# Two attentions: row maxima two groups ahead, and the first mask moved from TensorE to VectorE

## The chip, the cores and the metric

The program runs on one core of one Trainium2 chip. The metric is the device time of one launch in microseconds (us), and lower is better.

## The reference

Four blocks follow each other on x of shape (8, 256, 256), each added to x: an attention over a context with a causal mask, a mixture of 16 experts with the two best per token, a second attention over the same context without a mask, and a mixture of 7 experts with a capacity and a shared expert. What matters here are the two attentions, each with 16 heads of 16 channels and 256 queries and 256 keys per batch element:

```python
scores = jnp.einsum('bhqd,bhkd->bhqk', q, k) / jnp.sqrt(jnp.float32(dk))
causal = jnp.triu(jnp.ones((q_len, k_len), dtype=bool), k=1)
scores = jnp.where(causal, NEG_INF, scores)          # first attention only
scores = jnp.where(attention_mask[:, None, :, :], NEG_INF, scores)
attn = jax.nn.softmax(scores, axis=-1)
out = jnp.einsum('bhqk,bhkd->bhqd', attn, v)
```

## The kernel before

`attend_block` builds one attention. It runs over 8 batch elements, called batches here, and in a batch over 4 groups (`NG`) of 4 heads (`G`), so 32 groups per attention. The five engines are programmed apart and meet at semaphores; the order of the work is written out by hand in one function `batch` for each engine. All engines execute their instructions in order.

Queries and keys are split in three bf16 parts each (`split`, on VectorE for the first ones, on GpSimd after that), stored to DRAM (`store_parts`) and loaded back as stacks of 96 rows (`load_stack`, 12 transfers of 128 KB per batch: 6 of `ks<-parts` and 6 of `qs<-parts`). There are two stacks, used in turn: the loads for batch f go into the stack that batch f-2 used, so SyncE waits for the last transposed scores of batch f-2 (semaphore `scoredT`) and for the stores of the parts before it issues them. In the middle of batch n TensorE also makes the keys, queries and values of batch n+2 and the output of batch n-1, spread over the 16 heads ("slots") by `feed`. The queries of batch n+2 are made in slots 7 and 8, taken by ScalarE in slot 9 and then split by GpSimd.

Each group goes through these steps.

- `score` (TensorE, L984 and L986): scores with queries on the partitions, from the 96 rows. It writes one unit at a time into two PSUM banks used in turn; a unit is four heads by 128 keys or two heads by 256 keys, 3 units per group in the first attention and 4 in the second. In the first attention each product is followed by a second matmul that adds the mask `shut` through an identity.
- `reduce` (VectorE, L639): one `tensor_reduce` per unit takes the row maxima into PSUM. A unit may be scored when the reduce of the unit two before it is done (`reduced`).
- `tops` (VectorE, L647 and L649): splits the maxima in two bf16 parts.
- `turn_tops` (TensorE, L997): transposes them into a PSUM bank that the transposed scores use too.
- ScalarE copies them as rows 96 to 104 of the stack of queries (L882).
- `scoreT` (TensorE, L1016 and L1018): per head the scores with keys on the partitions, from 104 rows, so that the row maximum is subtracted by the matmul; in the first attention the mask is added by a second matmul. Two banks in turn.
- ScalarE takes the exponential (L892), `value` (TensorE, L1032) multiplies by the values, ScalarE copies out (L855, `take`), `turn_o` (TensorE) transposes, `normalize` (VectorE, L658 to L664) divides by the sum.

Before the change these run one group apart: in group g, TensorE scores the units of group g+1 and turns the maxima of group g. Its order within a group is the one of the lines below; `more` is false in the last group alone.

```python
score_next(0)
turn_tops(at)
if started:
    value(prior(at))
score_next(1)
scoreT(at, 0)
...
scoreT(at, 3)
```

Since `score_next` in group 3 belongs to the next batch, the stack of that batch is waited for there (`stacks_loaded`). In the first batch of the first attention VectorE also takes the moments (`moments`, L627) of the tiles to come, and their averages close its group 1; GpSimd waits for them (`root`), and the split of the queries of batch 2 stands behind that.

## Time and profile before

| | us |
|---|---|
| runs of the kernel, median (lowest, highest) | 1265.51 (1264.04, 1271.85) |
| profiled execution, span from first to last instruction | 1262.1 |
| first attention, about | 0 to 220 |
| second attention, about | 500 to 693 |

| engine | busy us | share of the span |
|---|---|---|
| TensorE, matmul | 1123.7 | 89% |
| TensorE, weight load | 974.6 | 77% |
| VectorE | 690.8 | 55% |
| ScalarE | 595.9 | 47% |
| GpSimd | 360.7 | 29% |

The span comes from one execution taken with the profiler, and it has no other time of its own; what lies around the instructions is taken as the difference to the median, 3.4 us. Busy times of matmuls overlap each other, so a high share does not say how much a matmul costs; the distance between two starts does.

### The profile page before, as it was taken

What the parts mean: (1) busy time and instruction counts of PE and PEld (TensorE: products, weight loads), DVE (VectorE), ACT (ScalarE), POOL (GpSimd) and SP (SyncE); (2) the same over time, 40 slices, a digit from 0 to 9 for tenths busy, and PEclk for the clock granted to TensorE, in tenths of its full rate; (3) what the DMA queues carried; (4) which work ended last, traced back from release to release, by engine and by line L of the source; (5) the groups of instructions that cost most, each with busy time, mean ns of one, the idle gap of its engine ahead of it and who ended that gap; (6) DMA issues with size and microseconds to landing.
All of it is one profiled execution on the core that took longest, in us unless ns stands there. A gap on an engine that the chain in (4) does not pass through costs nothing. (4 is left out here: it accounts for less than half of the span.)

```text
span 1262.1 us, 25941 instructions
## 1 busy us (share of the span) xinstructions
PE 1123.7 (89%) x8539; PEld 974.6 (77%) x8539; DVE 690.8 (55%) x1558; ACT 595.9 (47%) x1211; POOL 360.7 (29%) x502
## 2 busy tenths in 40 slices
PE   5999998739999984888998679999999999999997
PEld 4788786329888873555665379999999999999996
DVE  4755666652222226676767655555556555555556
ACT  3566666313222222776787334444445444444432
POOL 6566650112222205776630145000000000000261
PEclk8899999859999996999999879999999999999999
DMA  7774461548999957568471221223232232232132
GB/s 182 175 180 120 129 179 37 193 159 292 332 330 325 314 207 163 111 136 146 89 125 24 100 89 59 79 63 112 72 103 76 87 109 87 86 100 73 50 97 80
DMA packets 88137, 172.56 MB, mean 137 GB/s; under 512 B 11251, under 2 KB 59949, under 8 KB 81792
## 3 DMA queue, kind: packets, MB, share of 16 engines
q1 hardware_dynamic: 71712, 136.15, 39.0%
q0 software_dynamic: 9584, 29.32, 7.9%
q10 hardware_dynamic: 6768, 6.16, 1.4%
q8 instruction: 40, 0.66, 0.2%
q14 instruction: 33, 0.27, 0.1%
HBM read 133.11 MB, written 39.20 MB: 137 GB/s over the span
## 5 line engine op out<-in xcount | busy, mean ns | idle before, releaser
L2136 PE MATMUL e_ps<-xT_e,wp_e 128*128 128x384 f32 (+1 forms) x1344 | 245.2, 331 | 4.0 <-DVE wp_e L2010 4.0
L2136 PEld LDWEIGHTS e_ps<-xT_e,wp_e 128*128 128x128 f32 x1344 | 221.7, 188 | 5.4 <-issue 4.1
L639 DVE TENSOR_REDUCE att_ps<-att_ps 128x2 f32<-128x512 f32 (+1 forms) x224 | 155.3, 697 | 103.5 <-PE att_ps L986 63.2
L1968 ACT ACTIVATE act_a_e<-e_ps 128x256 f32<-128x256 f32 (+2 forms) x176 | 77.8, 442 | 159.9 <-PE e_ps L2136 150.9
L2066 DVE TENSOR_TENSOR hid_e<-act_a_e,e_ps 128x256 f32<-128x256 f32 (+2 forms) x176 | 87.0, 494 | 116.6 <-ACT act_a_e L1968 102.4
L892 ACT ACTIVATE probs<-att_ps 128x384 f32<-128x384 f32 (+1 forms) x256 | 130.4, 546 | 41.4 <-PE att_ps L1018 29.0
L1972 ACT ACTIVATE hidp_e<-hid_e 128x256 fp32r<-128x256 f32 (+2 forms) x176 | 83.8, 476 | 127.3 <-DVE hid_e L2066 121.5
L2153 PE MATMUL e_ps<-wp_e,hidp_e 128*128 128x256 f32 (+1 forms) x1008 | 138.4, 282 | 2.9 <-DVE xres L2026 1.2
L2068 DVE TENSOR_TENSOR hidp_e<-hid_e,hidp_e 128x256 fp32r<-128x256 f32 (+2 forms) x176 | 87.8, 499 | 95.5 <-ACT hidp_e L1972 90.1
L2153 PEld LDWEIGHTS e_ps<-wp_e,hidp_e 128*128 128x128 f32 (+1 forms) x1008 | 130.7, 183 | 4.9 <-issue 4.1
L1608 ACT ACTIVATE hid_e<-e_ps,b_ahead 128x128 f32<-128x128 f32 x188 | 53.7, 368 | 139.9 <-PE e_ps L1713 129.2
L1919 POOL DMA_DIRECT2D done<-y_e x7 | 6.2, 893 | 384.3 <-DVE y_e L2050 384.3
L984 PE MATMUL att_ps<-ks,qs 96*128 96x256 bf16 (+1 forms) x512 | 102.4, 267 | 11.4 <-DMA qs<-parts 9.5
L2136 PE MATMUL e_ps<-xT_e,swp_e 128*128 128x256 f32 x768 | 106.0, 289 | 1.5 <-issue 0.8
L1016 PE MATMUL att_ps<-qs,ks 104*128 104x256 bf16 (+1 forms) x512 | 99.7, 262 | 3.4 <-ACT qs L882 1.5
L1713 PEld LDWEIGHTS e_ps<-xT_e,w_e 128*128 128x128 f32 x752 | 89.9, 194 | 16.5 <-issue 15.3
L2136 PEld LDWEIGHTS e_ps<-xT_e,swp_e 128*128 128x128 f32 x768 | 98.5, 195 | 2.8 <-DVE swp_e L2005 2.3
L1713 PE MATMUL e_ps<-xT_e,w_e 128*128 128x128 f32 x752 | 94.4, 279 | 6.4 <-DMA w_e<-in_W 5.8
L1589 POOL DMA_INDIRECT x_e<-rows,owner_e x47 | 44.7, 952 | 168.7 <-PE e_ps L1703 125.1
L882 ACT ACTIVATE qs<-att_ps 8x1024 bf16<-8x1024 f32 x64 | 65.1, 1017 | 52.9 <-PE att_ps L997 52.0
L1722 PE MATMUL e_ps<-w_e,hid_e 128*128 128x256 f32 x376 | 88.9, 380 | 0.0
L984 PEld LDWEIGHTS att_ps<-ks,qs 96*128 96x128 bf16 x512 | 48.0, 100 | 39.7 <-issue 20.7
(235 smaller groups left out, 1850.0 us busy)
## 6 DMA issues: line engine op xcount, KB each, us to landing
w_e<-in_W SPq DMA_DIRECT2D x47, 1024.0 KB
w_e<-in_W SPq DMA_DIRECT2D x57, 384.0 KB, 3.1
ks<-parts SPq DMA_DIRECT2D x96, 128.0 KB, 4.7
qs<-parts SPq DMA_DIRECT2D x96, 128.0 KB, 5.2
parts<-cut SPq DMA_DIRECT2D x30, 384.0 KB, 3.2
x_e<-rows SPq DMA_DIRECT2D x8, 768.0 KB, 5.6
done<-y_e ACTq DMA_DIRECT2D x47, 128.0 KB
rows<-zeros POOLq DMA_DIRECT2D x8, 736.5 KB, 6.6
```

The source lines that it names most:

```text
L639: dve.tensor_reduce(tops_at(at[3])[:, qt, x0:x0 + heads], src, AX.X, ALU.max).then_inc(reduced, 1)
L892: act.activation(probs[:, g % 2, x0, 0:WIDE], ps[:, TB + x0 % RING, 0:WIDE], ACT.Exp, scale=DK ** -0.5).then_inc(exped, 1)
L984: last = pe.matmul(out, qs[0:KS, j, hd, qt * P:(qt + 1) * P], ks[0:KS, j, hd, 0:keys(qt)], start=True, stop=not causal)
L1016: last = pe.matmul(out, ks[:, j, hd, kt * P:(kt + 1) * P], qs[:, j, hd, q0:S], start=True, stop=not causal)
L1713: last = pe.matmul(ps[:, HB + j % 2, f * P:(f + 1) * P], w1(j, c, f), xT[:, j % 2, c, :], start=c == 0, stop=c == DC - 1)
L1722: last = pe.matmul(ps[:, YB + j % 2, 0:D], hid[:, j % 2, f, :], w2(j, f), start=f == 0, stop=f == FC0 - 1)
L1968: act.activation(act_a[:, u % 2, 0:n], ps[:, AB + u % 2, 0:n], ACT.Silu).then_inc(silu_ready, 1)
L1972: act.activation(hidp[:, u % 2, 0, 0:n], hid[:, u % 2, 0:n], ACT.Copy).then_inc(hid_high, 1)
L2066: dve.tensor_tensor(hid[:, u % 2, 0:n], act_a[:, u % 2, 0:n], ps[:, BB + u % 2, 0:n], ALU.mult).then_inc(mixed, 1)
L2068: dve.tensor_tensor(hidp[:, u % 2, 1, 0:n], hid[:, u % 2, 0:n], hidp[:, u % 2, 0, 0:n].bitcast(F32), ALU.subtract).then_inc(hid_cut, 1)
L2136: last = pe.matmul(ps[:, bank + u % 2, 0:n], weights(lot, c, pw)[:, (b * DC + d) * P:(b * DC + d + 1) * P], xT[:, px, d, t0:t0 + n], start ...
L2153: last = pe.matmul(out, hidp[:, u % 2, px, t * P:t * P + rows], weights(lot, c, pw)[:, 2 * DC * P:], start=c == 0 and q == 0 and tile % 2 ...
```

## The change

Both attentions: VectorE and TensorE now work on the maxima of group g+2 while group g is in hand. Two groups are scored and reduced ahead of the first batch, `score_next` takes `after(after(at))`, and the maxima are held in SBUF (`row_tops`). The turned maxima get a PSUM place of their own, in the bank where the maxima stood, and ScalarE copies them for group g+1 in the middle of group g (`set_rows`), between the second and the third exponential. `value` moves from before the first transposed scores to behind the second, `turn_o` behind the fourth.

First attention: the mask matmul of `score` is gone (the one of `scoreT` stays). VectorE adds the mask to each head's scores and takes the maximum with one `tensor_tensor_reduce` per head, 8 per group, where one `tensor_reduce` per unit stood, 3 per group.

```diff
-            return ps[:, MB, (g % 2) * TPB * G:(g % 2 + 1) * TPB * G].rearrange("p (t x) -> p t x", t=TPB)
+            return row_tops[:, g % 2]
...
             def reduce(at, u):
                 qt, x0, heads = UNITS[u]
                 dve.wait_ge(scored, ready(group(at) * NU + u))
+                if causal:
+                    if at[3] == 0 and u == 0:
+                        dve.wait_ge(shut_ready, at[0] + 1)
+                    for x1 in range(heads):
+                        col = x1 * 512 // heads
+                        last = dve.tensor_tensor_reduce(out=closed_scores[:, qt, x0 + x1, 0:keys(qt)], in0=ps[:, unit_bank(at, u), col:col + keys(qt)],
+                                                        in1=shut[:, 0, at[0], qt, 0:keys(qt)], scale=1.0, scalar=MASKED, op0=ALU.add, op1=ALU.max,
+                                                        accum_out=tops_at(at[3])[:, qt, x0 + x1:x0 + x1 + 1])
+                    last.then_inc(reduced, 1)
+                    return
...
-                    more, started = not (last and g == NG - 1), not (first and g == 0)
+                    more, started = not (last and g >= NG - 2), not (first and g == 0)
...
-                            reduce(after(at), u)
+                            reduce(after(after(at)), u)
...
-                        tops(after(at))
+                        tops(after(after(at)))
...
-            for u in range(NU):
-                reduce((0, 0, 0, 0), u)
-            tops((0, 0, 0, 0))
-            if ye is None:
-                split(dve, 1, 0)
+            for g in range(2):
+                for u in range(NU):
+                    reduce((0, 0, 0, g), u)
+                tops((0, 0, 0, g))
+                if ye is None and g == 0:
+                    split(dve, 1, 0)
...
-                    act.wait_ge(top_turned, ready(group(at)))
-                    act.activation(qs[KS:KT, j, g * G:(g + 1) * G, :], ps[KS:KT, TB, 0:S].unsqueeze(1).to_broadcast([2 * G, G, S]),
-                                   ACT.Copy).then_inc(row_ready, 1)
-                    if not (first and g == 0):
-                        take(prior(at))
...
+                        if x0 == 1:
+                            if not (first and g == 0):
+                                take(prior(at))
+                            if not (last and g == NG - 1):
+                                set_rows(after(at))
...
-                    last = pe.matmul(out, qs[0:KS, j, hd, qt * P:(qt + 1) * P], ks[0:KS, j, hd, 0:keys(qt)], start=True, stop=not causal)
-                    if causal:
-                        last = pe.matmul(out, m["identb"][:], closed(n, 0, qt, 0, keys(qt)), start=False, stop=True)
+                    last = pe.matmul(out, qs[0:KS, j, hd, qt * P:(qt + 1) * P], ks[0:KS, j, hd, 0:keys(qt)], start=True, stop=True)
...
-                            score(after(at), u)
+                            score(after(after(at)), u)
...
                     score_next(0)
-                    turn_tops(at)
-                    if started:
-                        value(prior(at))
-                    score_next(1)
                     scoreT(at, 0)
                     feed(n, j, r, g * G)
...
                     scoreT(at, 1)
+                    if started:
+                        value(prior(at))
+                    score_next(1)
+                    feed(n, j, r, g * G + 1)
+                    if not (last and g == NG - 1):
+                        turn_tops(after(at))
+                    scoreT(at, 2)
                     score_next(2)
-                    feed(n, j, r, g * G + 1)
+                    feed(n, j, r, g * G + 2)
+                    scoreT(at, 3)
+                    score_next(3)
                     if started:
                         turn_o(prior(at))
-                    scoreT(at, 2)
-                    score_next(3)
-                    feed(n, j, r, g * G + 2)
-                    scoreT(at, 3)
                     feed(n, j, r, g * G + 3)
```

The queue of SyncE, with its stores and loads of the parts, is the same in both kernels.

TensorE before, first attention, batch 1: the end of group 2 (`wo,oT` is slot 11) and the first scores of batch 2, at the head of group 3.

```order
L1059 MATMUL att_ps<-wo,oT 128x256 x2
L977 REGISTER_ALU
L980 ISA [waits shut_ready_0,stacks_loaded0_0]
L984 MATMUL att_ps<-ks,qs 128x128 [waits reduced_0]
L986 ISA
L986 MATMUL att_ps<-shut,identb 128x128
L984 MATMUL att_ps<-ks,qs 128x128
L986 MATMUL att_ps<-shut,identb 128x128
```

TensorE now, same batch: the end of group 1 (`hT,wq` is slot 7) and the first scores of batch 2, at the head of group 2.

```order
L977 MATMUL att_ps<-hT,wq 128x256
L1005 REGISTER_ALU
L1006 ISA [waits stacks_loaded0_0]
L1010 MATMUL att_ps<-ks,qs 128x128 [waits reduced_0]
L1010 MATMUL att_ps<-ks,qs 128x128 x3
L1035 REGISTER_ALU [waits row_ready_0]
L1041 MATMUL att_ps<-qs,ks 128x256 [waits exped_0]
L1043 MATMUL att_ps<-shut,identb 128x256
L1041 MATMUL att_ps<-qs,ks 128x128
L1043 MATMUL att_ps<-shut,identb 128x128
L977 MATMUL att_ps<-hT,wq 128x256 x2
```

The wait for the stack of the next batch stands one group earlier, in front of the second half of the queries (slot 8), and the mask matmuls between the scores are gone.

VectorE before, ahead of the first batch of the first attention: the maxima of group 0, then the split of the queries of batch 1.

```order
L639 TENSOR_REDUCE att_ps<-att_ps 128x4 [waits scored_0]
L639 TENSOR_REDUCE att_ps<-att_ps 128x2 [waits scored_0] x2
L647 TENSOR_SCALAR top_parts<-att_ps 128x2x4
L649 SCALAR_TENSOR_TENSOR top_parts<-att_ps,top_parts 128x2x4
L327 CAST cut<-full 128x512 [waits q_taken_0]
```

VectorE now, the second half of the same group; the two units of two heads.

```order
L649 ISA closed_scores,row_tops<-att_ps,shut 128x256 [waits scored_0]
L649 ISA row_tops 128x1
L649 ISA closed_scores,row_tops<-att_ps,shut 128x256
L649 ISA row_tops 128x1
L649 ISA closed_scores,row_tops<-att_ps,shut 128x256 [waits scored_0]
L649 ISA row_tops 128x1
L649 ISA closed_scores,row_tops<-att_ps,shut 128x256
L649 ISA row_tops 128x1
L663 TENSOR_SCALAR top_parts<-row_tops 128x2x4
```

Each head's operation has become two instructions, the fused one and one that writes its maximum.

## Rows read from the trace of the kernel before

**Rows 1.** Windows: busy us of PE, PEld, DVE, ACT, POOL; PEclk, DMA share, GB/s.

```profile
100.00:150.00 50.00, 49.73 (x511) 40.42 (x509) 28.23 (x78) 33.43 (x63) 29.90 (x30) 1.00 0.51 135
...
550.00:600.00 50.00, 42.59 (x352) 28.45 (x353) 35.15 (x86) 34.62 (x62) 33.95 (x61) 0.97 0.68 128
```

**Rows 2.** Timeline of PE, first attention, batch 3 (start us, us, operation).

```profile
118.58 0.22 PE L984 MATMUL att_ps<-ks,qs 96*128 96x128 bf16 x1
118.64 0.22 PE L986 MATMUL att_ps<-shut,identb 128*128 x1
...
119.99 0.28 PE L984 MATMUL att_ps<-ks,qs 96*128 96x256 bf16 x1
120.11 0.28 PE L986 MATMUL att_ps<-shut,identb 128*128 x1
...
120.52 0.28 PE L1016 MATMUL att_ps<-qs,ks 104*128 104x256 bf16 x1
```

**Rows 3.** Groups by form, DVE: count, busy us, mean ns, idle us before.

```profile
L639 DVE TENSOR_REDUCE att_ps<-att_ps 128x2 f32<-128x512 f32 x192 | 133.2, 697 | 77.4 <-PE att_ps L986 37.1 <-PE att_ps L984 35.9 <-issue 1.3
...
L664 DVE TENSOR_TENSOR on<-att_ps,share 128x128 f32<-128x128 f32 x64 | 18.7, 292 | 5.0 <-issue 0.3
```

**Rows 4.** Timeline of DVE, first attention, the end of one group.

```profile
56.58 0.17 DVE L647 TENSOR_SCALAR top_parts<-att_ps 128x8 bf16<-128x8 f32 x1
56.82 0.17 DVE L649 SCALAR_TENSOR_TENSOR top_parts<-att_ps,top_parts 128x8 bf16<-128x8 f32 x1
56.91 0.16 DVE L658 TENSOR_SCALAR share<-att_ps 128x8 f32<-128x8 f32 x1
...
57.41 0.29 DVE L664 TENSOR_TENSOR on<-att_ps,share 128x128 f32<-128x128 f32 x1
```

**Rows 5.** Timeline of SP's queue: first issue behind the wait for batch f-2.

```profile
82.67 0.37 SPq L413 DMA_DIRECT2D cst<-in_ctxT  x1
...
106.97 0.37 SPq L413 DMA_DIRECT2D cst<-in_ctxT  x1
...
131.26 0.37 SPq L413 DMA_DIRECT2D cst<-in_ctxT  x1
...
179.94 3.72 SPq L139 DMA_DIRECT2D ks<-parts  x6
```

**Rows 6.** Tile qs on SP: loads of batches 2, 3 and 7, each with landing.

```profile
L139 SPq DMA_DIRECT2D qs<-parts x6: 436/500/1335, 65.6 to 69.1; - x6
DMA to landing us min/median/max: 5.9/6.5/7.4
...
L139 SPq DMA_DIRECT2D qs<-parts x6: 303/533/851, 87.0 to 90.4; - x6
DMA to landing us min/median/max: 4.2/4.5/4.8
...
L139 SPq DMA_DIRECT2D qs<-parts x6: 436/894/1526, 183.7 to 188.9; - x6
DMA to landing us min/median/max: 6.1/6.7/7.3
```

**Rows 7.** Timeline of PE, group 2 of batch 1, and group 3 of batch 6.

```profile
71.93 0.28 PE L1016 MATMUL att_ps<-qs,ks 104*128 104x256 bf16 x1
...
195.34 0.23 PE L984 MATMUL att_ps<-ks,qs 96*128 96x128 bf16 x1 [0.62 <-DMA qs<-parts]
```

**Rows 8.** Timeline of POOL, first attention: root in batch 0, query splits.

```profile
48.10 0.26 POOL L390 TENSOR_SCALAR spread<-mean_var 128x10 f32<-128x10 f32 x1 [1.48 <-DVE mean_var L632]
...
57.71 1.16 POOL L333 TENSOR_TENSOR cut<-rest,cut 128x512 bf16<-128x512 f32 x1
...
125.45 1.16 POOL L333 TENSOR_TENSOR cut<-rest,cut 128x512 bf16<-128x512 f32 x1
```

**Rows 9.** Timelines, second attention: PE in batch 2, POOL in batch 2.

```profile
578.14 0.61 PE L984 MATMUL att_ps<-ks,qs 96*128 96x256 bf16 x2 [3.73 <-DMA qs<-parts]
...
582.18 1.16 POOL L333 TENSOR_TENSOR cut<-rest,cut 128x512 bf16<-128x512 f32 x1
```

More of the change, by code:

```diff
@@ L213, in attend_block @@
         if causal:
+            closed_scores = sb("closed_scores", [P, TPB, G, S], BF16)
             shut = sb("shut", [P, 2, B, TPB, S], BF16)
@@ L305, in place, with turned_tops @@
             return bank + f if early(f) else XB
+        def turned_tops(lo, hi):
+            return ps[KS:KT, MB, lo:hi]
         def tops_at(g):
[L309 removed]
+            return row_tops[:, g % 2]
         def comes(n, kind):
@@ L789, in _ @@
                 split(dve, 1, 1)
-            for u in range(NU):
-                reduce((0, 0, 0, 0), u)
-            tops((0, 0, 0, 0))
-            if ye is None:
-                split(dve, 1, 0)
-            batches(dve, batch)
+            for g in range(2):
[4 more added lines that the diff above has]
+                    split(dve, 1, 0)
+            if causal:
+                for n in range(B):
+                    batch(n, n % 2, n // 2, n == 0, n == B - 1)
+            else:
+                batches(dve, batch)
             normalize((B - 1, 1, None, NG - 1))
@@ L894, in batch, with set_rows @@
                             norm_rows(n + FEED, j, H_SLOTS.index(slot))
+                        if x0 == 1:
[3 more added lines that the diff above has]
+                                set_rows(after(at))
+            def set_rows(at):
+                n, j, r, g = at
+                act.wait_ge(top_turned, ready(group(at)))
+                act.activation(qs[KS:KT, j, g * G:(g + 1) * G, :], turned_tops(0, S).unsqueeze(1).to_broadcast([2 * G, G, S]),
+                               ACT.Copy).then_inc(row_ready, 1)
             def square_root(f, n, k):
@@ L926, in _ @@
                 act.activation(warm[:], offset[:, 0:1], ACT.Exp)
+            set_rows((0, 0, 0, 0))
             batches(act, batch)
@@ L994, in turn_tops @@
                 pe.wait_ge(top_ready, ready(group(at)))
-                pe.wait_ge(exped, free(n * H + g * G))
                 for t in range(TPB):
-                    last = pe.matmul(ps[KS:KT, TB, t * P:(t + 1) * P], top_parts[:, g % 2, t].rearrange("p a g -> p (a g)"),
+                    last = pe.matmul(turned_tops(t * P, (t + 1) * P), top_parts[:, g % 2, t].rearrange("p a g -> p (a g)"),
                                      m["identb"][:], start=True, stop=True, tile_position=(0, KS))
@@ L1006, in scoreT @@
                     pe.wait_ge(row_ready, ready(group(at)))
+                if x0 == 0 and g == 0 and causal:
+                    pe.wait_ge(shut_ready, n + 1)
                 if x0 == 0 and g == 0:
@@ L1101, in batch @@
                     at = (n, j, r, g)
-                    more, started = not (last and g == NG - 1), not (first and g == 0)
+                    more, started = not (last and g >= NG - 2), not (first and g == 0)
                     def score_next(u):
                         if more and u < NU:
-                            score(after(at), u)
+                            score(after(after(at)), u)
                     if first and g == NG - 1 and ahead is None:
@@ L1169, in _ @@
                 score((0, 0, 0, 0), u)
+            score((0, 0, 0, 1), 0)
+            turn_tops((0, 0, 0, 0))
+            for u in range(1, NU):
+                score((0, 0, 0, 1), u)
             batches(pe, batch)
```

3 lines of the change are left out of this document (1 added, 2 removed).

## The prediction

> **What bounds the kernel now.** I read the windows first. In the first attention TensorE is busy for 49.7 of 50 us with the clock at 1.00, while VectorE has 28 and ScalarE 33; in the second it is busy for 42.6, with VectorE at 35 [rows 1]. The timeline of TensorE shows what a matmul really costs there: a score over 128 keys and its mask start 0.06 apart, over 256 keys 0.12 apart [rows 2], so the first attention is a nearly closed chain of TensorE work. Then I read the queue of SyncE, because the change moves a wait for a transfer. The issues behind the last transposed scores of a batch stand at 82.67, 106.97 and 131.26 [rows 5]: one batch takes 24.3 us, a group 6.1. Last comes the question of when the stacks land and when they are asked for. In batch 6 of the first attention and in batch 2 of the second TensorE already waits for them, at the head of group 3, 0.6 and 3.7 us [rows 7, 9]. So two chains lie close to each other in both attentions: TensorE's own work, and the loop of last score, load, first score of the next batch, and the rest of the batch.
>
> **What goes from TensorE.** Eight mask matmuls per group, four at 0.06 and four at 0.12, are 0.72 us, in 32 groups 23 us [rows 2]. Most of the small waits for maxima at the head of a group go as well, perhaps 0.3 of them per group. By itself this makes a batch of 24.3 us one of 24.3 - 4 x 0.72 - 4 x 0.3 = 20.2. The same rows give such a matmul a duration of 0.22 to 0.28 us; by that the gain would be 256 x 0.25 = 64 us. The Trainium skill ("Perfetto Trace Analysis", Identifying the Most-Contended Engine) says that matmul busy time does not show how near TensorE is to its limit, since the instructions are pipelined. The trace agrees with it, as the starts are 0.06 to 0.12 apart, and the 23 us stand.
>
> **What comes to VectorE.** Three reduces of 0.70, 2.1 us per group, become eight fused operations and eight instructions that write the maximum. The trace has none of either. An operation on 128 elements out of PSUM takes 0.29 and one on 512 takes 0.70 [rows 3], so 1.05 ns per element, and 256 make 0.43. A tiny operation that need not wait for the one in front starts 0.09 behind it [rows 4]. I take 4 x 0.29 + 4 x 0.43 + 8 x 0.09 = 3.6 us per group: the operands are those of the 0.29 row. From below: the write costs nothing, 2.9. From above: two cycles per element, which puts 256 at the 0.70 of a 512 row and 128 at 0.43, and the write at a whole tiny instruction of 0.17 [rows 4], 4 x 0.43 + 4 x 0.70 + 8 x 0.17 = 5.9. Less than 2.1 is excluded, since three operations had the same elements with fewer fixed parts. Two parts of the maxima and the normalization are 1.1 us [rows 4], and residual and statistics some 2.5 per batch. VectorE then needs 4 x (3.6 + 1.2) + 2.5 = 21.7 us per batch, 18.9 from below, 31 from above. The Trainium skill ("VectorE: DVE Perf Modes", Rules for kernel authors) advises to keep the count of operations small rather than to fuse; the fused form raises the count from 3 to 16, and the rows of 0.29 and 0.70 agree that each operation has a fixed part of some 0.16.
>
> **The wait that is moved.** The first scores of batch n+2 now stand at the head of group 2 of batch n+1 and no longer of group 3. Nothing brings the loads forward: they still go out behind the last transposed score of batch n. From that release to the landing it takes 90.4 + 4.5 - 82.67 = 12.2 us for batch 3, and 195.3 - 179.94 = 15.4 for batch 7 [rows 5 to 7]; five batches are loaded so, and I take 13.2, nearer to the first, because only the last has its issues at a median of 894 ns [rows 6]. Without a wait TensorE would be at group 2 already 2 x 20.2 / 4 = 10 us after the release, so it waits 2 to 5 us in each batch. What is left from there is the stretch 120.52 to 131.26, 10.7 us [rows 2, 5]; the masks of five score units in it (1.1 us) go, and the 0.24 us of the scores in front come to it: 9.9. A second branch is as long at most: the second half of the queries stands just behind the wait, so their split, which ended at 126.61 [rows 8], keeps its 6.1 us behind 120.52, and its store was through by 131.26. The loop is then 13.2 + 9.9 = 23.1 per batch, against 24.3. Of the 4 us per batch that TensorE saves, 1.2 remain.
>
> **Its start.** The averages that release `root` on GpSimd at 48.10 [rows 8] stand behind three groups of reduces before and behind four after. VectorE gets 3 x (3.6 - 2.1) + 3.6 + 0.5 = 8.6 us more, less about 2 in which it waited: +6.5. Root, the split of the queries (end 58.87), store and loads follow directly, so the stack of batch 2 lands 6.5 later than at 69.1 + 7.4 = 76.5 [rows 6, 8], at 83.0. It is now asked for by group 2 of batch 1, whose transposed scores stood at 71.93 [rows 7]: 83.3 - 71.9 = +11.4 us. After it come five loops at -1.2, -6.0; the end of batch 6, which sheds five units' masks, -0.8; the last batch, with one group of scores fewer (1.35) and two groups of masks (1.4), and some waits less, -3.3. A wait of 9 us at batch 1, and one or two of 4 to 5, also let the clock fall: in the second attention, behind a wait of 3.7, two score matmuls took 0.61 us [rows 9], where at a clock of 1.00 the second starts 0.12 behind the first and takes 0.28, 0.40 together [rows 1, 2]. I put 3 us on that. First attention: 11.4 - 6.0 - 0.8 - 3.3 + 3 = +4.3 us.
>
> **Second attention.** No matmul goes. Here GpSimd is what the stacks wait for: the split of the queries for batch 4 ends at 583.34, at the end of batch 2, and the stack that was stored one such period earlier is there at 578.14 [rows 9]. TensorE will be at the head of group 2 at that time, where it now is at the head of group 3: one group of about 6 us behind. Against it stands the idle share, 7.4 of 50 us [rows 1], 0.9 per group. The lead takes away the part that waits for maxima, a sixth to a third of it; 0.2 in 20 groups behind that place gives 4 back. +2 us.
>
> **Sum.** +4.3 + 2 = +6.3, and about 3 more for the doubled prologue (a second group is reduced, 2.8 to 3.6 us, before the first transposed scores can start, in both attentions, of which part is hidden behind loads): +9. The profiled execution has a span of 1262.1, and with the 3.4 us around it this is the median of 1265.5; the forecast is 1271.1 of span and 1274.5 of time.
>
> **The rivals.**
> - *The stacks come in time and TensorE's saving is kept.* For it: GpSimd and SyncE have idle time, and a landing of 4 us [rows 6] leaves room if the queue drains faster. Against it: TensorE already waits for stacks at group 3 [rows 7, 9], and they are now asked for a group earlier. It would give -23 of masks, -8 of waits, +3 of prologue: 1237.5.
> - *VectorE becomes the bound of the first attention.* The price of the fused operation decides: from 3.95 us per group on, VectorE's batch exceeds the 23.1 of the loop. At the upper end of 5.9 it is 31, so +6.7 for 7 batches, +47 beside the second attention's +5: 1317; halfway, at 4.8 per group, 26.5 per batch, +2.2 for 7 batches and the same +5: 1286. For it: 16 instructions instead of 3. Against it: plain operations on these operands have the short time [rows 3].
> - *Both cancel to nothing.* If the start costs 4 and not 11 us, since VectorE catches up in its idle time, the sum is near +1: 1266.
>
> **How the numbers follow.** The forecast has 0.5, the cancelling 0.2, the kept saving 0.1, VectorE as the bound 0.2. The time is 1274.5. The range goes down to 1253, half way to the kept saving, and up to 1293, past the half-way price of VectorE. This kernel can tell about 1% from no change, 12.7 us. Faster by more: the kept saving and a little of the cancelling, 0.12. Slower by more, above 1278.2: VectorE's 0.2 and somewhat over a third of the forecast's own spread, 0.38. Between: 0.5.
>
> **What would show it.** In the changed profile TensorE's first score matmul of group 2 of most batches waits for `qs<-parts`, 2 to 5 us each, some 9 at batch 1; the same at group 2 of batches 1 to 3 of the second attention. The period of SyncE's loads is 22.5 to 24 us. `root` starts near 54 to 55. The fused operation reads 0.29 and 0.43, and VectorE's busy time goes up by about 32 x 1.5 = 48 us. The forecast is wrong if these waits are not there and the period is near 20, or if the waits are for VectorE and the period is above 25.

## The result and the profile after

The changed kernel takes 1323.19 us (median of 4 runs, 1313.7 to 1328.04) against 1268.13 for the kernel before in the same comparison: a ratio of 1.0423, 95% interval 1.0387 to 1.0458. I had forecast 1274.5 with a range up to 1293, so the direction of the likeliest case was right and the size was not: the loss is some 55 us and not 9. The profiled execution has a span of 1323.1, 61 more than that of before. Two single runs far above the rest of their kernel, one of 25 of the kernel before beside e1 to e4 (3816 us) and one of ten of e4 (6096 us), are left out of the ratios. Windows of the changed kernel, with the columns of [rows 1]:

```profile
100.00:150.00 50.00, 40.79 (x381) 29.33 (x379) 29.37 (x155) 28.26 (x54) 26.15 (x25) 0.97 0.59 113
...
550.00:600.00 50.00, 39.72 (x284) 23.74 (x285) 32.72 (x70) 30.18 (x56) 34.28 (x67) 0.85 0.53 111
```

In the first attention TensorE, busy for 49.7 of 50 us before, now has 40.8, and VectorE is hardly busier than before (29.4 against 28.2), so neither of them is the bound. In the second attention the clock is down to 0.85. The groups of VectorE by form, which answer to [rows 3]:

```profile
L649 DVE CUSTOM_DVE_ANT_0 closed_scores<-att_ps,shut 128x256 bf16<-128x256 f32 x128 | 49.0, 421 | 42.8 <-PE att_ps L1010 41.6
...
L649 DVE CUSTOM_DVE_ANT_0 closed_scores<-att_ps,shut 128x128 bf16<-128x128 f32 x128 | 29.4, 286 | 27.5 <-PE att_ps L1010 27.4
...
L649 DVE DVE_READ_ACCUMULATOR2_ANT row_tops<- 128x1 f32 x256 | 21.2, 83 | 0.0
```

The durations of the fused operation are as forecast (0.29 and 0.42), but the timeline shows more than they do: the write of the maximum starts with the next head's operation, and the operations follow each other at 0.22 us.

```profile
111.82 0.29 DVE L649 CUSTOM_DVE_ANT_0 closed_scores<-att_ps,shut 128x128 bf16<-128x128 f32 x1 [4.11 <-PE att_ps L1010]
112.03 0.08 DVE L649 DVE_READ_ACCUMULATOR2_ANT row_tops<- 128x1 f32 x1
112.03 0.29 DVE L649 CUSTOM_DVE_ANT_0 closed_scores<-att_ps,shut 128x128 bf16<-128x128 f32 x1
```

Next SyncE's queue, first issue behind the last transposed score of a batch (batches 1 to 5), as in [rows 5], and the loads of the queries for batches 3 and 4, as in [rows 6]:

```profile
95.50 0.37 SPq L419 DMA_DIRECT2D cst<-in_ctxT  x1
...
125.48 0.37 SPq L419 DMA_DIRECT2D cst<-in_ctxT  x1
...
151.44 0.37 SPq L419 DMA_DIRECT2D cst<-in_ctxT  x1
...
178.67 4.29 SPq L139 DMA_DIRECT2D ks<-parts  x6
...
207.16 0.95 SPq L139 DMA_DIRECT2D ks<-parts  x2
```

```profile
L139 SPq DMA_DIRECT2D qs<-parts x6: 302/421/540, 100.1 to 102.8; - x6
...
DMA to landing us min/median/max: 6.3/7.0/8.3
...
L139 SPq DMA_DIRECT2D qs<-parts x6: 423/423/432, 130.0 to 132.3; - x6
...
DMA to landing us min/median/max: 5.8/7.0/7.7
```

The period was 24.3 in all batches and is now 30.0, 26.0, 27.2 and 28.5. The stacks land at 111.1 (102.8 + 8.3), 140.0, 165.4, 193.0 and 223.3. From release to landing that is 14.0 to 16.1 us, mean 14.9; from landing to the next release 14.4, 11.4, 13.3 and 14.2, mean 13.3. The short one is the one in which the clock stays up, as windows of 3 us behind the four landings show (columns as above):

```profile
111.00:114.00 3.00, 2.77 (x12) 2.14 (x13) 0.93 (x8) 0.49 (x1) 0.00 (x0) 0.56 0.02 5
140.00:143.00 3.00, 2.91 (x34) 2.10 (x34) 0.93 (x8) 1.54 (x4) 0.56 (x1) 1.00 0.03 9
165.50:168.50 3.00, 2.97 (x15) 2.27 (x16) 0.93 (x8) 0.72 (x2) 0.00 (x0) 0.58 0.01 3
193.00:196.00 3.00, 2.97 (x14) 2.25 (x15) 0.93 (x8) 0.53 (x2) 0.00 (x0) 0.54 0.05 15
```

At 1.00, the level of 2.4 GHz, TensorE gets through 34 matmuls; at 0.54 to 0.58, mostly at 1.2 GHz, through 12 to 15. TensorE had waited 3.6, 2.5, 2.0 and 2.3 us for these four stacks, so the length of the wait alone does not say when the clock falls: behind 2.5 us it stayed up. The two halves make the whole period: the loop of the prediction is there, and it is 28 us long instead of 23.1. TensorE's waits, the answer to [rows 7, 9] (timelines of both attentions, then the summed waits of the first one, 40 to 240):

```profile
106.47 1.13 PE L977 MATMUL att_ps<-hT,wq 128*128 128x256 f32 x4 [0.50 <-ACT oT L881]
111.23 0.55 PE L1010 MATMUL att_ps<-ks,qs 96*128 96x128 bf16 x4 [3.64 <-DMA qs<-parts]
...
593.32 0.60 PE L1010 MATMUL att_ps<-ks,qs 96*128 96x256 bf16 x2 [7.02 <-DMA qs<-parts]
```

```profile
PE att_ps L1010 <- DMA qs<-parts: 20.6, 6, 8.1
PE att_ps L1010 <- DVE row_tops L649: 5.8, 3, 3.2
PE att_ps L969 <- ACT full L861: 3.2, 6, 0.7
PE att_ps L977 <- ACT oT L881: 2.5, 5, 0.5
```

The first two lines are the pattern of batches 2 to 5: queries of slot 7, the wait, then the scores of the next batch, and the second half of the queries behind them. The six waits of the first attention are 2.1 in batch 0, none in batch 1, then 3.6, 2.5, 2.0, 2.3 and 8.1; the five of the second are 7.0, 0.5, 0.8, 1.5 and 4.7.

Where the 61 us of span are, by TensorE's first and last transposed scores of each attention in the two traces (before, after): the first attention starts at 36.7 and 41.3 (+4.6), it lasts 180.7 and 208.4 (+27.7), the stretch up to the second attention's first transposed score 291.8 and 301.7 (+9.9), the second attention 181.7 and 200.0 (+18.3), the rest 571.1 and 571.9.

### The profile page after: what moved, and what is told of

Read it like the earlier page. It is cut to its first block and busy times, and to the rows that moved or that the text cites. A ratio compares the mean times of both kernels' runs of the same rounds, so it can differ in the third digit from the quotient of the medians.

```text
span 1323.1 us, 25740 instructions
## 1 busy us (share of the span) xinstructions
PE 1136.0 (86%) x8283; PEld 957.7 (72%) x8283; DVE 720.7 (54%) x1974; ACT 594.5 (45%) x1211; POOL 361.1 (27%) x502
## 5 line engine op out<-in xcount | busy, mean ns | idle before, releaser
L1010 PE MATMUL att_ps<-ks,qs 96*128 96x256 bf16 (+1 forms) x512 | 91.9, 276 | 51.5 <-DMA qs<-parts 40.3
L649 DVE CUSTOM_DVE_ANT_0 closed_scores<-att_ps,shut 128x128 bf16<-128x128 f32 (+1 forms) x256 | 78.0, 354 | 70.2 <-PE att_ps L1010 69.1
L655 DVE TENSOR_REDUCE row_tops<-att_ps 128x2 f32<-128x512 f32 x128 | 86.2, 685 | 52.6 <-PE att_ps L1010 50.3
L1041 PE MATMUL att_ps<-qs,ks 104*128 104x256 bf16 (+1 forms) x512 | 108.2, 273 | 3.3 <-ACT probs L907 3.0
L1010 PEld LDWEIGHTS att_ps<-ks,qs 96*128 96x128 bf16 x512 | 39.9, 101 | 87.7 <-issue 42.5
```

The source lines that it names most:

```text
L649: last = dve.tensor_tensor_reduce(out=closed_scores[:, qt, x0 + x1, 0:keys(qt)], in0=ps[:, unit_bank(at, u), col:col + keys(qt)], in1=shut ...
L655: dve.tensor_reduce(tops_at(at[3])[:, qt, x0:x0 + heads], src, AX.X, ALU.max).then_inc(reduced, 1)
L1010: last = pe.matmul(out, qs[0:KS, j, hd, qt * P:(qt + 1) * P], ks[0:KS, j, hd, 0:keys(qt)], start=True, stop=True)
L1041: last = pe.matmul(out, ks[:, j, hd, kt * P:(kt + 1) * P], qs[:, j, hd, q0:S], start=True, stop=not causal)
```

## The experiments

Theory A is the loop (last transposed score, load, first score of the next batch, rest of the batch). Rivals: B, VectorE's new work or the place of the maxima; C, the new order inside a group. Line numbers differ a little between kernels.

**e1: fused, but one group ahead.**

```diff
-                    last = pe.matmul(out, qs..., ks..., start=True, stop=not causal)
-                    if causal:
-                        last = pe.matmul(out, m["identb"][:], closed(n, 0, qt, 0, keys(qt)), ...)
+                    last = pe.matmul(out, qs..., ks..., start=True, stop=True)
...
+                        last = dve.tensor_tensor_reduce(...)
```

> The kernel before with the fused mask and maximum on VectorE alone: eight fused operations per group in the first attention, maxima of that attention in SBUF, still one group ahead, second attention as before. Theory A (the stack is asked for a group earlier, and that wait is the cost): this part is a gain, 8 masks of 0.72 us in 32 groups, so 1243 to 1252. Theory B (the fused operations and the maxima in SBUF hold VectorE and TensorE up): slower than before, 1280 or more. Theory C (the new order within a group, with value and turn_o later, is the cost): as A, 1243 to 1252.

Measured: 1259.91 us, ratio 0.9939 (0.9906 to 0.9972). The VectorE half of the change by itself is a small gain. It is well under the 23 us of masks, so it is in none of the ranges: A and C had it too fast, B too slow. One candidate stood in its trace, VectorE above and GpSimd below:

```profile
129.78 0.17 DVE L661 TENSOR_SCALAR top_parts<-row_tops 128x8 bf16<-128x8 f32 x1
130.03 2.12 DVE L663 SCALAR_TENSOR_TENSOR top_parts<-row_tops,top_parts 128x8 bf16<-128x8 f32 x1
```

```profile
130.00 2.12 POOL L369 TENSOR_TENSOR shut<-shut,later 128x1024 bf16<-128x1024 bf16 x1
```

With the maxima in SBUF this tiny operation of two SBUF inputs lasts exactly as long as GpSimd's one, and TensorE waits 1.12 us for it. The Trainium skill ("SBUF — State Buffer", SBUF: two separate sides) says that a VectorE operation with two SBUF inputs and a GpSimd operation that reads SBUF take one port pair in turn, each for its whole length; this row agrees. The other small operation, L661 with one input in SBUF, is held up as well: it lasts 2.07 us at 105.97, beside a GpSimd operation of 2.12 that starts at 105.89. Whether that was the lost gain is tested by e5.

**e2: two groups ahead, mask matmul and plain reduce kept.** The changed kernel with the old `reduce` and the old mask matmul in `score`.

```diff
-                if causal:
...
-                        last = dve.tensor_tensor_reduce(...)
...
+                    if causal:
+                        last = pe.matmul(out, m["identb"][:], closed(n, 0, qt, 0, keys(qt)), start=False, stop=True)
```

> The changed kernel with the mask back on TensorE and one tensor_reduce per unit, so two groups ahead alone. A: the loop of last score, load and first score holds the period, and the masks fill only a part of its waits: 1320 to 1340. B: without the fused operations the loss goes, 1265 to 1280. C: 1315 or more, as A.

Measured: 1325.72, ratio 1.0438 (1.0378 to 1.0499), the same as the whole change. The loss comes with the order alone, and with that order the fused operation gains nothing that shows. B falls. A and C both had this time; e3 and e11 separate them.

**e3 and e4: no stack loads from batch 2 on,** in the changed kernel and in the one before.

```diff
-                for w in KINDS:
-                    load_stack(sp, stacks[w], j, parts_dram, w, f, stacks_loaded[j])
...
-                    pe.wait_ge(stacks_loaded[j], 16 * len(STACK_Q) * 2 * (r + 1))
+                    if isinstance(n, int) and n < 2:
+                        pe.wait_ge(stacks_loaded[j], 16 * len(STACK_Q) * 2)
```

> The changed kernel without the loads of the stacks of batches 2 to 7 in both attentions and without the waits for them, so those batches are computed from the stacks of batches 0 and 1. A: all waits for stacks go with what follows from them, 1235 to 1255. B and C: the waits of VectorE or of the order stay, 1285 or more.

> The kernel before with the same loads and waits left out. All theories: it waits for stacks only three or four times, so 1255 to 1263. Under A the changed kernel without loads is then 10 to 20 us faster than this one, which is what the change is worth when stacks are free; under B and C it is slower than this one.

Measured: e3 1271.13, ratio 1.0032 (1.0004 to 1.006), between what A and its rivals said; e4 1263.09 (1262.3 without the run at 6096), 0.9953 (0.9924 to 0.9981), as expected by itself. Without the loads the changed kernel is 52 us faster and the kernel before some 5, so some 44 (by the ratios) to 47 of the 55 us hang on the loads of the stacks. With the order of two ahead still in place and that much gone, C is not the main cause. But under A e3 should have been 10 to 20 us below e4, and it is 8 to 10 above, though it lacks 23 us of masks. In the two profiled executions its first attention starts 3.4 us later and is only 2.6 shorter, the stretch between the attentions is 6.0 longer and the second attention 3.0. Its steady batches take 23.3 us where I had worked out 20.2; e4's take 24.3.

**e5: e1 with the maxima in PSUM.** In `tops_at` the PSUM place of before stands again.

```diff
-            if causal:
-                return row_tops[:, g % 2]
```

> The kernel before with the fused operation on VectorE in the first attention and no mask matmul in the scores, the maxima one group ahead and kept in PSUM (the earlier one-ahead kernel had them in SBUF). Theory A: one group ahead the 23 us of masks are there to be had, and that earlier kernel (1259.9) lost most of them to the small operations on maxima in SBUF, of which single ones took 1 to 2 us and TensorE waited for them. Then this one is at 1243 to 1256. Rival B: what held it back is the fused operation itself, eight short ones where three stood, in the chain score, maxima, transpose, rows within one group: then it stays at 1257 to 1263.

Measured: 1260.25, ratio 0.9933 (0.9909 to 0.9957). A fell: each of these small operations now lasts 0.165 to 0.168 us, and the time is the same as e1's. It is in B's range; whether for B's reason is the question of e6.

**e6: e5 without the stack loads.** The edits of e3 on e5.

```diff
-                for w in KINDS:
-                    load_stack(sp, stacks[w], j, parts_dram, w, f, stacks_loaded[j])
```

> As the kernel above (fused, one group ahead, maxima in PSUM), but the stacks of batches 2 to 7 are not loaded and not waited for, so these batches compute with the values of batches 0 and 1. The changed kernel without these loads took 1271, the kernel before without them 1263. Theory A: the stacks hardly cost the one-ahead order anything, so this is at most 6 us under the kernel above, and the masks show in full: 1238 to 1248. Then 23 to 33 us of the changed kernel are the order of two ahead itself, stacks or not. Rival B: the masks are worth little wherever the maxima are, because ScalarE or VectorE sets the pace once they are gone: 1258 to 1271.

Measured: 1251.84, ratio 0.9873 (0.9839 to 0.9908), between the two. Against e4 the masks are worth 10 to 11 us and not 23: a batch takes 22.8 us, against 24.3. The timelines show why. TensorE in e6, from the turning of the maxima (L1007) to the first transposed score (L1028):

```profile
132.46 0.39 PE L996 MATMUL att_ps<-ks,qs 96*128 96x128 bf16 x4
132.78 0.22 PE L1007 MATMUL att_ps<-identb,top_parts 128*8 128x128 bf16 x1
...
133.63 0.39 PE L996 MATMUL att_ps<-ks,qs 96*128 96x256 bf16 x2
134.16 0.28 PE L1028 MATMUL att_ps<-qs,ks 104*128 104x256 bf16 x1
```

and in e4, where these are L996 and L1015:

```profile
164.12 0.22 PE L996 MATMUL att_ps<-identb,top_parts 128*8 128x128 bf16 x1
...
165.32 0.27 PE L985 MATMUL att_ps<-shut,identb 128*128 128x256 bf16 x1
165.51 0.28 PE L1015 MATMUL att_ps<-qs,ks 104*128 104x256 bf16 x1
```

From turning to transposed score it is 1.38 us in e6 and 1.39 in e4. That is the time of the chain turn, copy by ScalarE (1.02 of it), score; the two masks of the unit in between (0.24 us) only filled it. Of 0.72 us per group 0.38 are left ((24.3 - 22.8) / 4); beside the 0.24, 0.1 stays unexplained.

**e7: in each group the first unit, and with it the wait, behind two transposed scores and the values.**

```diff
-                    score_next(0)
                     scoreT(at, 0)
...
                         value(prior(at))
+                    score_next(0)
                     score_next(1)
```

> The changed kernel, but in each group TensorE scores the first unit of the group two ahead behind two transposed scores and the values, instead of at the head of the group; so the wait for the next batch's stack, too, stands behind this work and behind the second half of the queries. Theory A (the loop of last transposed score, load, first score of the next batch, rest of the batch): what goes ahead of the wait, 2 to 3 us, leaves the loop in some 9 to 11 batches of both attentions: 1290 to 1308. Rival B: the waits for stacks are only where another lateness shows (ScalarE, VectorE or the small operations), or two units in a row make TensorE wait for VectorE: 1318 to 1335.

Measured: 1310.12, ratio 1.0328 (1.0296 to 1.036): 12 to 13 us back, just outside A's slow end and below all of B. The period of the loop is 25.3 in five batches, 12.9 to 14.1 to the landing and 11.2 to 12.4 from there: 2.6 us less than the changed kernel's mean of 27.9, as much as was moved ahead of the wait. But A had this in both attentions, and in the profiled executions the first one is 10.3 us shorter, the second 1.4 and the stretch between them 5.9.

**e8: TensorE kept busy ahead of the wait.**

```diff
+                    if not (isinstance(n, int) and n == 0):
+                        pe.wait_ge(reduced, free(group(at) * NU + u))
+                        for _ in range(64):
+                            pe.matmul(ps[:, unit_bank(at, u), 0:P], m["identb"][:], m["identb"][:], start=True, stop=True)
                     pe.wait_ge(stacks_loaded[j], 16 * len(STACK_Q) * 2 * (r + 1))
```

> The changed kernel with 64 small matmuls (128 columns, some 3.9 us at 0.06 each) into the free score bank ahead of each wait for a stack, batches 1 to 7 of both attentions; they compute nothing that is used. It prices the lowered clock behind the wait. Theory A: the stretch from landing to the next release, 11 to 14 us where I had worked out 9.9, is long because the clock is down to 0.56 for the first microseconds behind the wait: with it up, 1 to 2 us come back in each of some 11 loops, 1303 to 1313. Rival B: the stretch is long for what TensorE waits for in it, VectorE and ScalarE: 1318 to 1328, though the granted clock behind the wait is near 1. Where the stack is already there, the matmuls cost their 3.9 us.

Measured: 1322.51, ratio 1.0415 (1.0385 to 1.0446), no change in the total: A's 1303 to 1313 fell, and it is in B's range. Its window and timeline behind the wait for the stack of batch 4, which landed at 139.1:

```profile
139.00:143.00 4.00, 4.00 (x54) 2.94 (x51) 1.07 (x9) 1.85 (x4) 0.78 (x2) 1.00 0.04 11
```

```profile
136.16 3.74 PE L1008 MATMUL att_ps<-identb 128*128 128x128 bf16 x64
139.73 0.39 PE L1014 MATMUL att_ps<-ks,qs 96*128 96x128 bf16 x4
```

The clock is now at 2.4 GHz, and the stretch from the first transposed score of group 2 to the last one of the batch is 10.8 us in each of the batches 2 to 5, and 11.1 to the release. The changed kernel has 13.6, 10.8, 12.6 and 13.6 there, in the order of the windows above. But the matmuls end 0.6 us after the landing. The first attention's period is 26.9 (its length is 205.2, 3 less); the second attention is 7 longer. So the stretch is longer by 2.8, nothing, 1.8 and 2.8 us where the clock was down. Not all of that is the clock. In the first and the last of the four TensorE also waits 1.1 and 1.0 us for VectorE's residual, and rival B has its part there (VectorE above, TensorE below):

```profile
117.77 1.15 DVE L663 TENSOR_SCALAR top_parts<-row_tops 128x8 bf16<-128x8 f32 x1
118.99 1.04 DVE L665 SCALAR_TENSOR_TENSOR top_parts<-row_tops,top_parts 128x8 bf16<-128x8 f32 x1
```

```profile
122.24 1.13 PE L995 MATMUL att_ps<-wv,cst 128*128 128x256 f32 x4 [1.07 <-DVE xres L688]
```

Ahead of the residual stand the two small operations on the maxima, held up beside GpSimd's (1.16 at 117.73, then 2.77 at 118.97), where in the loop with the clock up they take 0.17 each. That leaves 1.7 to 1.8 us for the clock in each of the three slow loops. Paying for it with extra matmuls gives nothing in all.

**e9: e3 with the rows copied behind the third exponential; e10: the same in the changed kernel.**

```diff
                         if x0 == 1:
                             if not (first and g == 0):
                                 take(prior(at))
-                            if not (last and g == NG - 1):
-                                set_rows(after(at))
+                        if x0 == 2 and not (last and g == NG - 1):
+                            set_rows(after(at))
```

> As the changed kernel without the stack loads of batches 2 to 7 (1271), which computes these batches with the values of batches 0 and 1; and ScalarE copies the rows of the next group behind its third exponential instead of behind the second. In that kernel the copy of the rows takes ScalarE 1.0 us, after up to 0.9 of waiting for the turned maxima, and the copies of projections stand behind it, for which TensorE waits 0.5 us twice per batch, behind its transposes of the output. Theory A: this is what eats the saving of the masks: 0.7 to 1.3 us less per batch, 1253 to 1262. Rival B: ScalarE's order is not it, or the rows come late instead: 1267 to 1275.

> The changed kernel, all loads in place, with the same later copy of the rows. Theory A: the stretch from landing to the next release is long because of TensorE's waits for ScalarE in groups 2 and 3, so it shrinks by 0.5 to 1.2 in each of some 11 loops: 1308 to 1317. Rival B: the loop hides it, because the time saved in groups 0 and 1 only makes the wait longer and nothing of it lies behind the landing: 1319 to 1328.

Measured: e9 1271.59, ratio 1.0017 (0.9991 to 1.0044); e10 1332.78, ratio 1.0521 (1.0481 to 1.0562). Rival B of both, e10 even beyond it: its median is 10 us above that of the changed kernel, which no rival of mine had. The waits that I meant are real, as the timeline of e3 shows; but in every batch they stand at the ends of groups 0 and 1 (in the changed kernel at 101.42 and 106.47, for example), ahead of the wait for the stack and not behind it, as e10's theory had it:

```profile
120.85 0.39 PE L1066 MATMUL att_ps<-ident,o 128*128 128x128 f32 x2
121.74 0.44 PE L967 MATMUL att_ps<-ident,h 128*128 128x128 f32 x2 [0.50 <-ACT full L859]
```

and in e9 they are gone, with batches of 22.6 instead of 23.3. But the rows then come late (TensorE waits up to 0.8 us for `qs` from ScalarE), above all in batch 6, which takes 19.2 us where e3 has 17.8; and the second attention is 5 us longer, 183.2. The wait moved from one place to another.

**e11: two loads of the twelve.**

```diff
-    for r, part in enumerate((STACK_Q, STACK_K)[w]):
+    for r, part in enumerate((STACK_Q, STACK_K)[w][:rows]):
...
-                    load_stack(sp, stacks[w], j, parts_dram, w, f, stacks_loaded[j])
+                    load_stack(sp, stacks[w], j, parts_dram, w, f, stacks_loaded[j], range(PARTS), 1)
...
-                    pe.wait_ge(stacks_loaded[j], 16 * len(STACK_Q) * 2 * (r + 1))
+                    pe.wait_ge(stacks_loaded[j], 16 * len(STACK_Q) * 2 + 32 * r)
```

> The changed kernel, but from batch 2 on only the first of the six loads of each stack is issued (two of twelve per batch), so a part of each stack keeps old values. From release to landing it then takes some 6 to 8 us and no longer 14 to 16. Theory A: the loop is then 7 + 12 = 19 to 20 us, less than TensorE's own 23.3 per batch, and the waits go: 1268 to 1282, as without any loads. Rival B: a second branch is nearly as long, the one from the landing over the second half of the queries, their split and their store to the loads, or the splits on GpSimd set the landing: 1288 to 1312.

Measured: 1270.53, ratio 1.002 (0.9994 to 1.0047). The wait is still in the program, at the same place, with the same semaphores; only the transfer is shorter. SyncE's queue in e11, and the landing of the load of batch 4:

```profile
89.81 0.37 SPq L419 DMA_DIRECT2D cst<-in_ctxT  x1
...
113.11 0.37 SPq L419 DMA_DIRECT2D cst<-in_ctxT  x1
...
136.40 0.37 SPq L419 DMA_DIRECT2D cst<-in_ctxT  x1
```

```profile
L139 SPq DMA_DIRECT2D qs<-parts x1: 423/423/423, 114.0 to 114.0; - x1
...
DMA to landing us min/median/max: 5.8/5.8/5.8
```

From release (113.11) to landing it is 6.7 us instead of 14.0 to 16.1, the period is 23.3, that of e3, and no wait for a stack is left in the steady batches. This is the sharpest confirmation of A: the time goes with the length of the transfer, not with the wait as such. The branch over the second half of the queries does not bind at this period.

**e12: e5 with the third unit ahead of the first transposed score,** first attention.

```diff
                     score_next(1)
+                    if causal:
+                        score_next(2)
                     scoreT(at, 0)
```

> The kernel before with the fused operation, no mask matmul in the scores, maxima one group ahead and in PSUM (1260), and in the first attention the third unit of scores stands before the first transposed score instead of behind the second. There the first transposed score waits 0.25 to 0.5 us in each group for the rows of maxima, which the mask matmuls used to cover. Theory A: the unit fills this wait, 0.25 to 0.4 in 32 groups: 1247 to 1254. Rival B: the unit itself has to wait for VectorE to be through with the first one, whose bank it takes, and nothing is gained: 1257 to 1266.

Measured: 1264.63, ratio 0.9987 (0.996 to 1.0014). Rival B: TensorE now waits for VectorE instead, as its row shows, and the gain of e5 is gone.

```profile
132.92 0.39 PE L997 MATMUL att_ps<-ks,qs 96*128 96x256 bf16 x2 [0.56 <-DVE att_ps L644]
```

Of the kernels with all their loads only e1 and e5, one group ahead, are faster than the kernel before, by 0.6 to 0.7%.

## Why the prediction was wrong

**What went from TensorE.** The 23 us are right as a sum of distances: over three steady batches the scores with their masks take 18.1 us of TensorE's time in e4 and the scores alone 8.4 in e3, that is 3.2 per batch against my 2.9. The next sentence failed, "by itself this makes a batch of 24.3 us one of 20.2". It measured 23.3 (e3, e11), and 22.8 one group ahead (e6). The 4 x 0.3 for small waits were never there to be had: the 3.2 hold all that went, and [rows 1] had TensorE busy for 49.73 of 50 us. And 2.2 of the 3.2 came back in e3: 1.4 at the transposes of the output (`ident,o`), behind which TensorE now waits for ScalarE's copies, twice 0.5 us per batch with some 0.2 around each; 0.4 at the masks of the transposed scores; the rest in pieces of 0.2 and less. One group ahead the chain of rows over ScalarE took over (e6).

**What came to VectorE.** 3.6 us per group were forecast, the starts give 4 x 0.22 + 4 x 0.35 = 2.3. Even the bound from below (2.9) was too high, since the tiny write and the last 0.07 us of each operation lie beside the next one. VectorE's busy time went up by 30 us over the whole program (690.8 to 720.7) and not by 48. VectorE as the bound of the steady batches can be ruled out: it is busy for 59% of the stretch from 100 to 150 us, for 69% of the steady batches of e3, and e2, with the plain reduce, takes the same time. The advice cited in the prediction, to keep the count of operations small, has no price here: 16 instructions took about the time of the 3.

**The start.** The number is nearly right, the way to it is not, and that is luck. The averages came at 55.76 (forecast 54 to 55), 7.7 us later; but 4.6 of that is the later start of the attention, which I had booked under the prologue, and 3.1 is VectorE's part, for which I had 6.5:

```profile
55.76 0.26 POOL L396 TENSOR_SCALAR spread<-mean_var 128x10 f32<-128x10 f32 x1 [1.94 <-DVE mean_var L638]
```

The stack of batch 2 landed at 83.0, as worked out, and the transposed scores of group 2 of batch 1 stood at 84.4 instead of 71.9: +12.4 against +11.4. But TensorE did not wait for that stack, where I had a wait of some 9 us. It was late by itself and came 1.1 us behind the landing:

```profile
68.92 0.39 PE L1010 MATMUL att_ps<-ks,qs 96*128 96x256 bf16 x2 [3.18 <-DVE row_tops L649]
...
84.14 0.39 PE L1010 MATMUL att_ps<-ks,qs 96*128 96x128 bf16 x4
```

Its lateness grew from 4.6 us at the first transposed score to 8.0 at group 3 of batch 0, with 2.1 of waiting for the stack of batch 1, and to 10.8 at the start of batch 1, with 3.2 of waiting for VectorE. So here, outside the steady batches, VectorE did hold TensorE up. The 12.4 contain the 4.6 of the start.

**The wait that is moved.** This is the step that failed most. From group 2 of batch 1 to group 2 of batch 6 it is 139.4 us, 27.9 per loop, where before it was 118.8. I had -6.0 for the five loops, and they cost +20.6. Both halves of "13.2 + 9.9 = 23.1" were too short. Release to landing measured 14.9; read in the same way, the kernel before has 12.3 to 15.4, 13.4 on average, so the term was a fair reading of it and grew by 1.5. Landing to release measured 13.3 against 9.9, and there the reasoning was at fault: I took the masks off the stretch and did not ask what the new order brings into it. From the first transposed score of group 2 to the release it was 10.7 us; with the clock up it is 11.1 in the changed kernel (140.32 to 151.44) and in e8, and not 9.6. TensorE still sets this length, its starts stand in a closed row and no wait is named. The masks did go (1.1 us), but the `value` of group 2's turn came in. Before it stood ahead of the stretch, with the one of group 3 inside; now both are behind the landing. Before, then now:

```profile
119.25 0.81 PE L1032 MATMUL att_ps<-probs,v 128*32 128x256 f32 x13
```

```profile
142.01 0.86 PE L1057 MATMUL att_ps<-probs,v 128*32 128x256 f32 x16
...
147.19 0.86 PE L1057 MATMUL att_ps<-probs,v 128*32 128x256 f32 x16
```

By the distances of starts in e3 and e4 a `value` is 0.8 us. With it came one more unit of scores (0.25) and one more turning of maxima (0.4), and smaller shifts cancel. So what I had put at nothing ate the masks and 0.4 more; e7, which puts a `value` and more ahead of the wait again, shortened the loop by 2.6. Of the rest of the 13.3, 1.3 on average come from the clock, which was down behind three of these four waits, 0.5 from the waits for VectorE's residual in two of them (e8), and 0.3 to 0.5 us lies between the landing and the first transposed score, for which I had 0.24. I had put 3 us for the clock on the whole attention, while there are waits of this kind in every batch. The error fed itself: a loop longer than a batch's own work makes waits, and behind most of them the lower clock lengthened the loop by 1.7 to 1.8 us.

**Behind it,** from group 2 of batch 6 to the end of the attention, I had -0.8 and -3.3, and it is -0.8 in all.

**The second attention.** Forecast +2, measured +18.3. I let it be "one group of about 6 us behind" once. The loop runs there too: its batches take 23 to 34 us; from the release to the end of TensorE's wait it is 13.5 to 15.9 us in four batches, and from there to the next release 11.2 to 13.8. In e3, without the loads, the attention is 178.2 long against 181.7 before. It is not the loop alone: in two batches the loads go out 2.6 and 1.5 us behind the first issue, so that another wait of SyncE, by the program the one for the stores of the parts, ends last. That case did not need another experiment: I had written the loop down for one attention and not asked the same of the other.

**The prologue.** 3 us were forecast for both; 4.6 are in the first attention's start (3.0 on average over all traces, 40.4 with two groups ahead and 37.4 with one). VectorE is busy with the second group there and TensorE runs at 1.2 GHz. The window of the changed kernel, and below it the same of the kernel before:

```profile
36.00:42.00 6.00, 2.92 (x19) 1.37 (x16) 5.42 (x28) 1.02 (x1) 0.00 (x0) 0.50 0.82 190
```

```profile
36.00:42.00 6.00, 5.85 (x37) 4.37 (x36) 5.49 (x14) 3.85 (x8) 0.57 (x1) 0.78 0.88 137
```

The stretch between the attentions, which holds the other prologue, is 299.0 us on average over the eight two-ahead traces and 294.1 over the six one-ahead ones. Some 5 of the 9.9 us are therefore the change; the rest lies within what this stretch varies by, and what makes it vary stays open.

**The rivals.** "The saving is kept" does not even hold without the loads (e3, e11): the other half of its premise, that TensorE's own saving is real, was wrong too. "VectorE becomes the bound" came nearest in time (1286 to 1317), for the wrong reason. My test for it, "the forecast is wrong if the waits are for VectorE and the period is above 25", was half met: the period was above 25, with the waits for `qs<-parts`. A loop longer than 25 us had no case of its own. Two small slips in the numbers changed nothing: the sum for VectorE's batch takes 1.2 us for what its rows give as 1.1, and half way from the forecast to the kept saving is 1256 and not 1253.

Open: why e10 has a higher ratio than the changed kernel (1.0521 against 1.0423). In its profiled execution the first attention is 5 us shorter and the second 6 longer, and the span of 1322.0 is about the same; it is also the fastest of its four runs (1323.77, the others 1330.73 to 1335.43), so the trace does not show what they lose. Open too is what decides whether the clock falls in a wait of 2 to 4 us. And open is what makes the transfers 1.5 us longer.

## What to carry to other kernels

When a wait is moved, write down the whole loop that passes through it, for every stage that has the same structure, and list for each half what leaves it and what enters it: here 1.1 us of masks left the stretch behind the wait, and a reordering of the same change put 1.4 us into it. An instruction taken off an engine shortens only a stretch in which that engine is the last to be ready. A loop that comes out within a few per cent of the engine's own period is not a small risk, since the waits that it makes can lower the clock (to 0.54 to 0.58 behind three of four here) and lengthen the next lap; the cure tested here is a shorter transfer (e11), not a warm engine (e8). And a change of two parts is best priced apart: one part was worth 0.6 to 0.7%, the other cost 4%.

## What the runs showed of the hardware

- A `tensor_tensor_reduce` on VectorE with one operand in PSUM reads 0.286 us for 128 and 0.421 for 256 elements per partition, but such operations start 0.22 and 0.35 apart, and the second instruction that writes the accumulator (0.083) lies within that.
- Tiny VectorE operations (128x8) take 0.167 us on PSUM and 0.30 to 0.33 on average on SBUF, because single ones last until a GpSimd operation beside them is through: 1.17 us beside one of 1.16, 2.12 beside one of 2.12 (e1). TensorE waited 1.12 us for such a one, and the total was the same without them (e5).
- Two loads of 128 KB that are issued alone land 6.7 us after the release with a load of the context in front of them, and 3.9 and 4.9 without it (e11); twelve need 14.0 to 16.1 in the changed kernel and 12.3 to 15.4 in the one before.
- Behind waits of 3.6, 2.0 and 2.3 us TensorE's granted clock was 0.54 to 0.58 for 3 us, behind one of 2.5 it was 1.00. From the first transposed score to the release it was then 13.9, 12.9, 13.9 and 11.1 us; 1.1 of the first and 1.0 of the third are a wait for VectorE.
